# Routing logits and expert scores as column-group tiles, joined by a 0/1 product

## The reference

```python
# layer 0: which two experts
mixed = hidden_states @ wqkv.T                    # [384, 1024] @ [1024, 24]
q, k, v = jnp.split(mixed, 3, axis=-1)            # 8 columns each
attn = jax.nn.softmax(q[..., :, None] * k[..., None, :], axis=-1)
logits = jnp.einsum('bsej,bsj->bse', attn, v).reshape(-1, E)
top_logits, idx = jax.lax.top_k(logits, 2)
...
# layer 1: which one expert
aff = feats @ centroids.T                         # [384, 1024] @ [1024, 8]
eid = jnp.argmax(aff, axis=1)
```

## Time and profile before

| | us |
|---|---|
| median of 3 runs | 1029.05 (1028.74, 1029.05, 1031.53) |
| the profiled execution | 1027.06 |
| its span | 1025.1 |
| PE busy | 1001.5 (98%), 3591 instructions |
| DVE busy | 370.3 (36%) |
| ACT busy | 203.3 (20%) |
| POOL busy | 314.0 (31%) |

### The profile page before, as it was taken

One profiled execution on the slowest core, in us unless ns is written; L12 is line 12 of the kernel. 1 busy time (PEld: TensorE's weight loads), 2 busy tenths in 40 slices (PEclk: granted clock), 3 DMA queues, 4 the chain that ended last, 5 costly groups with the idle time before them and its releaser, 6 DMA issues.

```text
span 1025.1 us, 10404 instructions
## 1 busy us (share of the span) xinstructions
PE 1001.5 (98%) x3591; PEld 539.2 (53%) x3591; DVE 370.3 (36%) x1028; ACT 203.3 (20%) x416; POOL 314.0 (31%) x244
## 2 busy tenths in 40 slices
PE   5999999999999999999999999999999999999998
PEld 4555555555555544554456655544444455447432
DVE  6033563046300045840226111045203048667514
ACT  3123221111111115850012121121101110101320
POOL 2787887888788850000000000020000000000300
PEclk9999999999999999999999999999999999999999
DMA  9755445454544471002136989881522204728996
GB/s 327 200 98 149 129 108 145 102 135 101 125 104 101 102 236 62 1 21 103 53 120 231 339 318 356 298 315 42 185 102 103 102 21 160 275 91 279 387 366 249
DMA packets 63421, 172.76 MB, mean 169 GB/s; under 512 B 22176, under 2 KB 22912, under 8 KB 63248
## 3 DMA queue, kind: packets, MB, share of 16 engines
q1 hardware_dynamic: 38800, 146.56, 41.2%
q0 software_dynamic: 20528, 14.06, 7.8%
q10 hardware_dynamic: 4048, 11.59, 3.1%
HBM read 160.22 MB, written 11.95 MB: 168 GB/s over the span
## 4 chain that ended last, share of the span: by engine, by line
PE 85%; DMA 6%; DVE 3%; issue 3%; ACT 1%; SPq 0%; POOL 0%; ACTq 0%; DVEq 0%; POOLq 0%
PE bank L1055 36%; PE bank L1066 16%; PE bank L1042 9%; PE bank L1303 6%; PE bank L1518 3%; PE bank L1328 3%; DMA rows<-in_stream 2%; DMA Y<-in_stream 2%; PE bank L1156 2%; PE bank L1473 2%; PE bank L1630 1%; PE bank L1239 1%; PE bank L1649 1%; PE bank L1142 1%; DMA ys<-Y 1%
## 5 line engine op out<-in xcount | busy, mean ns | idle before, releaser
L1055 PE MATMUL bank<-xnT,ring 128*128 128x384 f32 x896 | 292.4, 487 | 1.2 <-ACT xnT L716 1.2
L1055 PEld LDWEIGHTS bank<-xnT,ring 128*128 128x128 f32 x896 | 169.6, 190 | 121.7 <-issue 3.6
L605 POOL DMA_INDIRECT Y<-xs,idx x8 | 7.7, 959 | 494.2 <-DMA xs<-Y 245.0
L551 POOL DMA_INDIRECT n_lo<-count,ridx x48 | 83.2, 1734 | 17.6 <-issue 13.7
L551 POOL DMA_INDIRECT n_hi<-count,ridx x48 | 80.2, 1671 | 17.5 <-issue 13.7
L1066 PE MATMUL bank<-ring,Y 128*128 128x512 f32 x192 | 83.9, 595 | 0.0
L1066 PE MATMUL bank<-ring,xnT 128*128 128x512 f32 x192 | 82.7, 592 | 0.0
L1055 PE MATMUL bank<-Y,ring 128*128 x256 | 82.7, 486 | 0.0
L1303 PE MATMUL bank<-ring,Y 128*128 128x352 f32 x256 | 77.4, 460 | 0.0
L740 ACT ACTIVATE Y<-bank,sbias,scale 128x384 f32 (+1 forms) x48 | 32.2, 670 | 202.3 <-PE bank L1055 183.6
L1055 PEld LDWEIGHTS bank<-Y,ring 128*128 128x128 f32 x256 | 48.6, 190 | 33.9
(11 more groups left out here) (355 smaller groups left out, 1106.3 us busy)
## 6 DMA issues: line engine op xcount, KB each, us to landing
ring<-in_stream SPq DMA_DIRECT2D x144, 512.0 KB
ring<-in_up SPq DMA_DIRECT2D x32, 704.0 KB, 5.6
Y<-in_stream SPq DMA_DIRECT2D x18, 512.0 KB, 10.8
G<-in_stream SPq DMA_DIRECT2D x16, 512.0 KB, 6.8
ring<-in_dn SPq DMA_DIRECT2D x7, 1024.0 KB, 5.9
rows<-keys SPq DMA_DIRECT2D x10, 512.0 KB
ys<-Y ACTq DMA_DIRECT2D x9, 512.0 KB, 7.6
xnT<-in_stream SPq DMA_DIRECT2D x6, 512.0 KB, 9.9
```

Of the source, the lines that this page charges most:

```text
L551: pool.indirect_dma_start(table, bass.IndirectOffsetOnAxis(ap=at[:, e:e + 1], axis=0), what[:, e:e + 1], None, **how).then_inc(done, 16)
L605: pool.indirect_dma_start(dst, None, src, bass.IndirectOffsetOnAxis(ap=idx[:, col:col + 1], axis=0))\
L1055: last = pe.matmul(bank[to][:, 0:N], ring[:, r, k * P:(k + 1) * P], rhs(k), start=(k == 0), stop=(k == KB - 1))
```

## The change

The narrow matrix becomes the weights and the tokens stream. Each chunk k has its own product: weights are 32 columns of the stored matrix from column k*n on (n is 24 or 8; the columns beyond the chunk's own n belong to the next chunk or to a zeroed pad), the 128 tokens stream, and the result goes to 32 partitions of the bank. Chunk k takes column group k mod 4, so four chunks stand on four column groups and chunks k and k + 4 accumulate on one group. The bank then holds four partial sums, transposed, each 32 partitions high and 128 tokens wide. ACT copies them to SBUF (`evict_parts`), and one more product with the copy as weights and a 0/1 matrix `by_group` (1 where partition mod 32 is the column) adds the four groups and turns the result back into 128 tokens x 24 or 8 (`join_logits`, `join_affinities`). The wait counters used for this are two that had been counted to 2 before. The stored matrices get a pad that DVE zeroes at the start, the constants get 24 columns more.

The joins stand on PE: in layer 0 of block 0 after slots 4 to 7 of block 1, of block 1 after slot 4 of block 2, of block 2 directly after its parts; in layer 1 of block 0 after slot 4, of block 1 after slot 5, of block 2 directly after its parts. The copies on ACT stand right after the evictions of the same block.

```diff
+            def evict_parts(dst, n, b):
+                act.wait_ge(parts_ready, n + b + 3)
+                act.activation(dst, bank[2 if b < NB - 1 else 5][:, P:2 * P], ACT.Copy).then_inc(parts_taken, 1)
...
                 seed(1 + b, b, b + 1)
                 evict_block(TP0, b)
+                evict_parts(logit_parts, 0, b)
                 store_normed(b)
...
             evict_half(TP0, NB - 1, 1)
+            evict_parts(logit_parts, 0, NB - 1)
             act.wait_ge(act_input, GM)
...
             for b in range(NB - 1):
                 seeds(b)
                 evict_block(TP0 + 4 * NB, b)
+                evict_parts(score_parts, NB, b)
...
             evict_block(TP0 + 4 * NB, 2)
+            evict_parts(score_parts, NB, 2)
             both_seeds(2)
...
+            def parts_of(W, n, b, half):
+                for k in range(4 * half, 4 * half + 4):
+                    g = 32 * (k % 4)
+                    last = pe.matmul(logit_bank(b)[g:g + 32, P:2 * P], W[:, k * n:k * n + 32], xtok(k, b),
+                                     start=(half == 0), stop=(half == 1), skip_group_check=True)
+                return last
+
             def raw_logits(b, half):
                 pe.wait_ge(t_evicted, T_LN2 + 2 * b + half + 1)
-                to = bank[2][:, b * 24:(b + 1) * 24] if b < NB - 1 else bank[5][:, 0:24]
-                for k in range(4 * half, 4 * half + 4):
-                    last = pe.matmul(to, xtok(k, b), wqkv[:, k, :], start=(k == 0), stop=(k == KB - 1))
-                if half and b:
+                last = parts_of(gates, 3 * NE, b, half)
+                if half:
+                    last.then_inc(parts_ready, 1)
+
+            def join_logits(b):
+                pe.wait_ge(parts_taken, b + 3)
+                last = pe.matmul(logit_bank(b)[:, b % 2 * 24:b % 2 * 24 + 24], logit_parts, by_group, start=True, stop=True)
+                if b:
                     last.then_inc(pe_output, 1)
...
                     block_rows(b, range(4, 8), tok(4), arrived, False, True)
-            block_rows(NB - 1, range(4, 7), tok(4), arrived, False, False)
+                    join_logits(b - 1)
+            block_rows(NB - 1, range(4, 5), tok(4), arrived, False, False)
+            join_logits(NB - 2)
+            block_rows(NB - 1, range(5, 7), tok(4), arrived, False, False)
             rank_rows(R0, 0, NB - 1)
...
             raw_logits(NB - 1, 1)
+            join_logits(NB - 1)
...
             block_rows(2, range(4, 5), tok(2), 0, True, False)
+            join_affinities(0)
             for half in range(2):
                 affinities(1, half)
-            block_rows(2, range(5, 7), tok(2), 0, False, False)
+            block_rows(2, range(5, 6), tok(2), 0, False, False)
+            join_affinities(1)
+            block_rows(2, range(6, 7), tok(2), 0, False, False)
             rank_rows(R1, 0, NB - 1)
...
             for half in range(2):
                 affinities(2, half)
+            join_affinities(2)
...
+            v.memset(gates[:, 3 * NE * KB:], 0.0)
+            v.memset(centers[:, NE * KB:], 0.0)
             rstds(0, xr, lambda b: v.wait_ge(x_in[b], 16 if b else 32))
```

More of the change, by code:

```diff
@@ L197, in program @@
         dst16 = sb("dst16", [P, ET], F16)
-        wqkv = sb("wqkv", [P, KB, 3 * NE])
-        cent = sb("cent", [P, KB, NE])
+        gates = sb("gates", [P, 3 * NE * KB + 8])
+        centers = sb("centers", [P, NE * KB + 24])
+        wqkv = gates[:, 0:3 * NE * KB].rearrange("p (k n) -> p k n", k=KB)
+        cent = centers[:, 0:NE * KB].rearrange("p (k n) -> p k n", k=KB)
         idx = sb("idx", [P, 48], U32)
@@ L227, in program @@
         hbase = k32[:, 691:715]
+        by_group = k32[:, 715:739]
         iota = k16[:, 0:384]
@@ L321, in program @@
         stored = sem("stored")
+        parts_ready, parts_taken = keys_ready, beta_exp
         edge_rows = mask[0:ET, 0, 0:2 * P].bitcast(I32).rearrange("p (a n) -> p a n", a=2)
@@ L358, in program @@
         first_rows = mask[:].rearrange("p b n -> p (b n)")[:, 512:512 + N].rearrange("p (b n) -> p b n", b=NB)
+        logit_parts = mask[:].rearrange("p b n -> p (b n)")[:, 0:P]
+        score_parts = Y[:, 1, 2816:2816 + P]
         first_pair = Y[:, 1, 2432:2432 + N].rearrange("p (b n) -> p b n", b=NB)
@@ L724, in _ @@
             act.activation(spw[:, 1, :], spw[:, 3, :], ACT.Ln).then_inc(act_output, 1)
-            act.dma_start(wqkv[:], wqkv_d).then_inc(biases_and_gates_in, 16)
-            act.dma_start(cent[:], cent_d).then_inc(biases_and_gates_in, 16)
+            act.dma_start(wqkv, wqkv_d).then_inc(biases_and_gates_in, 16)
+            act.dma_start(cent, cent_d).then_inc(biases_and_gates_in, 16)
             def evict_T(layer, m):
@@ L1212, in turn_raw, with logit_bank @@
                 last.then_inc(tp_ready, 1)
+            def logit_bank(b):
+                return bank[2 if b < NB - 1 else 5]
+            def parts_of(W, n, b, half):
[4 more added lines that the diff above has]
+                return last
             def raw_logits(b, half):
                 pe.wait_ge(t_evicted, T_LN2 + 2 * b + half + 1)
-                to = bank[2][:, b * 24:(b + 1) * 24] if b < NB - 1 else bank[5][:, 0:24]
-                for k in range(4 * half, 4 * half + 4):
-                    last = pe.matmul(to, xtok(k, b), wqkv[:, k, :], start=(k == 0), stop=(k == KB - 1))
-                if half and b:
+                last = parts_of(gates, 3 * NE, b, half)
[5 more added lines that the diff above has]
+                if b:
                     last.then_inc(pe_output, 1)
@@ L1543, in affinities, with join_affinities @@
                 pe.wait_ge(t_evicted, T_FE + 2 * b + half + 1)
[L1544 to L1547, removed]
+                last = parts_of(centers, NE, b, half)
+                if half:
+                    last.then_inc(parts_ready, 1)
+            def join_affinities(b):
+                pe.wait_ge(parts_taken, NB + b + 3)
+                last = pe.matmul(logit_bank(b)[:, b % 2 * NE:b % 2 * NE + NE], score_parts, by_group[:, 0:NE],
+                                 start=True, stop=True)
+                if b:
                     last.then_inc(pe_output, 1)
@@ L2005, in _ @@
             step(ts(ahead, ahead, -1.2e-38, None, ALU.mult))
-            step(v.tensor_reduce(small_sums, wqkv[:].rearrange("p k n -> p n k"), AX.X, ALU.add))
+            step(v.tensor_reduce(small_sums, wqkv.rearrange("p k n -> p n k"), AX.X, ALU.add))
             v.wait_ge(bias_added, NB)
@@ L2300, in _ @@
             step(stt(xf, Y[:, 5, :], -1.0, xf, ALU.add, ALU.add))
-            step(v.tensor_reduce(cent_sums, cent[:].rearrange("p k n -> p n k"), AX.X, ALU.add))
+            step(v.tensor_reduce(cent_sums, cent.rearrange("p k n -> p n k"), AX.X, ALU.add))
             step(ts(cent_sums, cent_sums, -1.0, None, ALU.mult))
@@ L2483, in constants @@
     ebase = np.tile(np.arange(NE, dtype=f) * CAP, (P, NB))
-    c32 = np.concatenate([ident, bd, headcol, later, np.ones((P, P), f), iota8, ebase, beyond, same, ebase / 2], 1)
+    c32 = np.concatenate([ident, bd, headcol, later, np.ones((P, P), f), iota8, ebase, beyond, same, ebase / 2,
+                          part % 32 == np.arange(3 * NE)[None, :]], 1).astype(f)
     token = np.arange(N).reshape(NB, P).T
```

## The result

| | before | after |
|---|---|---|
| median | 1030.32 us (17 runs, 1028.17 to 1035.21) | 1034.25 us (17 runs, 1029.27 to 1036.83) |
| ratio | | 1.0033, 95% interval 1.0021 to 1.0045 |
| the profiled execution | 1027.06 us, span 1025.1 | 1033.72 us, span 1031.9 |
| mean granted clock in it | 1.000 | 0.998 |

By the ratio the change costs 3.4 us (by the two medians 3.9). The 1031.4 that was predicted is 2.9 too low against the median, and the range's upper end, 1034.2, is passed by 0.05. Two things are in these 2.9: the median of before is 1030.32 over 17 executions and not the 1029.05 of the three that the forecast started from (1.3), and the change costs more than the 2.3 that was forecast. With the ratio put on the forecast's own 1029.05 it would be 1032.4.

What follows compares the result with a forecast made beforehand. PE was taken as the chain nearly everywhere, except block 2's ends. Layer 0 +0.1, layer 1 +2.4 and w2 -0.2 make +2.3: 1029.4 against the profiled 1027.06, 1031.4 with the median 2.0 above; range 1028.5 to 1034.2.

Steps and rivals of the forecast that it cites:

- Price of a visit: One block's products with the narrow matrix on PE: 0.79 us in tiles instead of 1.70, 0.91 saved.
- The join: Two full f32 passes on PE between out-projection passes: 0.14 to 0.21 us, 0.21 taken.
- Layer 0: First routing: PE's saving is given back as a 1.5 us wait before rank; +0.1 us in all.
- Block 2: End of layer 0's routing, evictions to DVE's first reading: 1.30 us instead of 1.23, +0.07.
- Layer 1: Second routing: ACT's copy of block 0's parts holds back block 1's seed, reciprocal +5.97 us; +2.4 us in all.
- almost 3 us: PE's gap before layer 1's transposes of block 1, waiting for DVE's halves of x; a sign of being right.
- After it: After layer 1's routing the delay moves on; PE's 0.7 us wait for the last w2 chunk takes back 0.2.
- PE's clock falls: Rival: PE's stop at 922 in layer 1 lowers the clock, 3 us more, 1034.4; chance 0.08.
- The cover holds: Rival: neither rank nor seed holds PE in either routing; -2.3 us, 1026.8; chance 0.15.

Runs made afterwards that it cites:

- joins early: After with block 1's and 2's square roots ahead of ACT's copies (layer 1), blocks 0/1's visits one slot earlier, joins one slot behind (layer 0): 1026.97, ratio 0.9971.
- after's second trace: The kernel after, unchanged, profiled again; the clock holds behind PE's 2.21 us stop: 1030.04 us.
- joins early in layer 1 too: Joins early, plus layer 1's block 0 visit after the first slot, its join two slots later, block 1's second seed behind the copy: 1027.33, ratio 0.9966.
- layer 1 alone: After with layer 0's logits put back to the products of before, without joins there: 1031.35, ratio 1.0019.

## Why the prediction came out as it did

- *Price of a visit*: right. Predicted 0.79 and 0.91 saved, measured 0.74 and 1.04 (before, 1.78 with the same count). Four groups do run beside each other: 16 passes are over in 0.57, where four groups in turn would need 1.70. By the rule of the Trainium skill (TensorE: Matmul & The Clock Gate, Part 3, The mechanism) the weight loads of tiles that share their rows don't overlap the running matmuls, and by the prediction's estimate from that page the visit would be 0.43 longer, 1.22; the trace disagrees with it here as it did at the K-V product.
- *The join*: 0.21 taken, 0.14 measured, the lower of its two ends.
- *Layer 0*: right, +0.1 predicted. Measured from the out-projection pass at 510.92 before and 510.40 after, the routing is as long as before (39.66 in four traces, 39.69 and 39.67 in the two of after without a fall there), DVE's reading comes 0.13 later (+0.32 predicted), PE waits 1.28 (1.5), and rank comes 0.14 earlier (+0.05). What was saved is given back as a wait, as said; joins early show it, since without the wait the routing is shorter by 1.4. Block 2: from the end of the evictions (541.76) to DVE's reading 1.38, priced 1.30, 1.23 before.
- *Layer 1*: the mechanism was right to the instruction, the size a little high. Counted from the start of the blocked fc product, 914.76 before and 915.38 in after's second trace: reciprocal +5.87 (predicted +5.97); next fc pass behind the transposes +1.49 (+1.59); DVE's reading +2.78 (+3.18); DVE's last half of block 2 +1.42 (+1.9); block 2's first choice +1.91 (+2.4). The gap of "almost 3 us" is 2.21, because the transposes of the first half start when DVE has done one half of x; the pass behind them is only 0.1 from its forecast.
- *After it*: 0.2 was to be taken back by the w2 landing. The end's own scatter, 1.7 us in four traces of one kernel, hides that.
- *What was missed*: the sum, +2.3, was to be the whole, and the change costs 3.4 by the ratio. By the landmarks of after's second trace, in which the clock holds, it is -0.2, +0.9, +1.9 and -0.3 against the averages of before, together +2.3. That this equals the forecast is luck: 0.9 of it, between the routings, was put at nothing without a reason, layer 1 is 0.5 less than forecast, and the first and the last figure are scatter. (The executions at full clock say +1.9; for after they are only five.) The rest is *PE's clock falls*, a rival with a chance of 0.08. It was put as an event that happens or doesn't: "3 more, 1034.4". In truth it is a chance in every execution, before the change too (41 of 79), and a median over executions contains it. The profile after shows what the prediction named as a sign of being wrong, a clock under 1.00 near 925 (0.91 and 0.50 from 926 to 930); two other traces of after don't. Seen behind the stop in one trace of three, it cost 1.4 there, not 3, as the clock was low for some 3 us in which PE's passes of 0.43 took twice as long. The time of the rival, 1034.4, is near the median, but by luck: the falls in layer 0, behind a gather and behind the w2 landing weren't thought of, since the profiled execution of before has 1.00 everywhere. Why after loses more of its clock, 1.7 us on average, isn't shown. The stop is one place where it fell, but the kernel with layer 1's change alone has the stop and fell in 5 of 12 executions only.
- *The cover holds* (1026.8) didn't hold, and by its mechanism: the seed and the rank. With both repaired the two routings are together 2.9 shorter (1.4 and 1.5), and 3.2 with the joins early in layer 1 too (1.4 and 1.7), where -2.3 was worked out with a visit and a join that both came out cheaper. The whole is at 1026.4 and 1026.5 at full clock against 1028.90, -2.5: near the rival's figure, though 0.5 to 1.0 of what the routings gain is lost between them.

## What to carry to other kernels

A copy that one engine makes for a later step has a place in that engine's program, and what stands behind it waits for its input too: before adding it, ask what the engine must deliver next, and put the copy behind that. Here that order was worth 2.7 us in layer 1's routing, nearly what the tiles of both layers save in both routings once nothing waits (2.9 to 3.2). A saving on the engine of the chain can be lost again at the next thing that this engine waits for, as in layer 0 here; starting the producer earlier brought it back. A profile shows one execution: where its clock is 1.00 throughout, the list of all executions says how often it isn't.

## What was not expected of the hardware

- Four column groups with 128 rows each and f32 weights of 32 columns: 16 passes of 128 columns in 0.57 us from the first start to the next full load, 0.036 a pass, where one alone streams 0.107.
- Behind a stop of PE of 2.2 to 2.6 us the clock fell in three traces (2.2 in after, 2.6 at a gather, 2.3 at w2) and stayed at 1.00 in three (2.2 in after's second and third trace and in layer 1 alone). In four of the fourteen traces it fell near 543.5, where no single wait is over 0.9 us; two of these have PE idle 1.27 us at 536 to 538 and two do not.
- A store of 512 KB is seen by the gather behind it after 7.8 to 8.2 us in four traces of before and after 8.8 in all three of after (8.2 to 9.0 in the other kernels), with no instruction of that stretch changed.
